# Short attention units: probabilities normed on VectorE before their transposition, in place of an inverse row fetched through DRAM

## The reference

```
B, T, M, D, G, H = 2, 1024, 256, 128, 4, 4
q = rope(einsum('bim,ghmd->bghid', x, w_aq)); k = rope(einsum('bim,gmd->bgid', x, w_ak))
v = einsum('bim,gmd->bgid', x, w_av)
s = einsum('bghid,bgjd->bghij', q * D ** -0.25, k * D ** -0.25)
s = s - 1e30 * (i < j)
p = softmax(s, axis=-1)
o = einsum('bghij,bgjd->bghid', p, v)
r = einsum('bghid,ghdm->bim', o, w_ao)
x = layernorm(x + r)
x = layernorm(x + moe(x))
```

## Time and profile before

| | |
|---|---|
| three runs | 1063.52 to 1064.9 us, median 1064.26 us |
| the profiled execution | 1066.87 us, span of its instructions 1065.0 us |
| TensorE's clock, mean of the span | 0.958 of full speed |
| busy share of the span | PE 89%, DVE 67%, ACT 49%, POOL 42% |

### The profile page before, as it was taken

How to read it: one execution, slowest core, us unless ns; L and a number is a source line. 1 busy time by engine, 2 the same in 40 slices (tenths; PEclk the granted TensorE clock), 3 DMA queues, 4 the chain that set the end, 5 groups by cost and what they waited for, 6 DMA issues and landing times.

```text
span 1065.0 us, 17542 instructions
## 1 busy us (share of the span) xinstructions
PE 950.3 (89%) x5448; PEld 733.9 (69%) x5448; DVE 710.2 (67%) x1751; ACT 517.4 (49%) x1139; POOL 447.2 (42%) x390
## 2 busy tenths in 40 slices
PE   8999996979999999999968899999999999478744
PEld 6887875756788878777756667888778777245411
DVE  5989863757767676767657877677777676433326
ACT  4111133545656656565656556556566655134402
POOL 3878872244342414124257534424132231325711
PEclk9999998989999999999999999999999999679968
DMA  8786766422334211211234235321212033999687
GB/s 241 234 265 226 258 227 178 131 94 78 99 88 121 64 50 46 68 40 61 66 103 122 71 95 135 92 75 42 70 42 61 26 108 87 257 260 224 87 280 285
DMA packets 137306, 137.28 MB, mean 129 GB/s; under 512 B 18065, under 2 KB 108805, under 8 KB 137216
## 3 DMA queue, kind: packets, MB, share of 16 engines
q1 hardware_dynamic: 84064, 98.33, 30.0%
q10 hardware_dynamic: 43872, 29.50, 9.3%
q0 software_dynamic: 9280, 8.34, 4.2%
HBM read 86.44 MB, written 63.05 MB: 140 GB/s over the span
## 4 chain that ended last, share of the span: by engine, by line
PE 68%; DVE 9%; issue 7%; DMA 7%; POOL 3%; SPq 3%; ACT 2%; ACTq 1%; POOLq 0%; DVEq 0%
PE s_ps L1193 16%; PE ring L1203 10%; PE o_ps L1223 10%; PE o_ps L1220 7%; PE s_ps L1172 6%; PE ring L1242 6%; PE ring L1172 5%; DMA sums<-erow,goal_u 3%; SPq L811 2%; PE o_ps L1172 2%; DVE neg_max L1407 2%; PE ring L1233 2%; PE s_ps L1196 1%; POOL slot_rows L909 1%; DMA fsum<-sums 1%
## 5 line engine op out<-in xcount | busy, mean ns | idle before, releaser
L1038 ACT ACTIVATE probs<-s_ps,neg_max 128x128 f32<-128x128 f32 (+7 forms) x256 | 189.4, 740 | 118.8 <-DVE neg_max L1407 110.4
L1193 PE MATMUL s_ps<-kt,qt_hi 128*128 128x512 f32 (+3 forms) x768 | 230.9, 382 | 5.1 <-issue 2.4
L1407 DVE TENSOR_REDUCE neg_max<-s_ps 128x1 f32<-128x128 f32 (+7 forms) x256 | 191.5, 751 | 57.4 <-PE s_ps L1196 55.6
L1203 PE MATMUL ring<-ident,probs 128*128 128x128 f32 x1152 | 177.1, 277 | 19.1 <-ACT probs L1038 10.4
L1193 PEld LDWEIGHTS s_ps<-kt,qt_hi 128*128 128x128 f32 x768 | 137.4, 192 | 50.5 <-issue 29.4
L938 ACT ACTIVATE pt_hi<-ring 128x512 fp32r<-128x512 f32 x168 | 100.1, 596 | 141.1 <-PE ring L1203 138.6
L881 POOL TENSOR_TENSOR ot_lo<-ot_raw,ot_hi 128x512 fp32r<-128x512 f32 x52 | 66.7, 1283 | 240.1 <-ACT ot_hi L938 240.1
L1341 DVE TENSOR_TENSOR pt_lo<-ring,pt_hi 128x512 fp32r<-128x512 f32 x168 | 115.6, 689 | 67.9 <-ACT pt_hi L938 65.4
L1203 PEld LDWEIGHTS ring<-ident,probs 128*128 128x128 f32 x1152 | 128.8, 142 | 43.6 <-issue 24.3
L1223 PE MATMUL o_ps<-pt_hi,v 128*128 128x512 f32 x336 | 144.2, 430 | 0.0
L886 POOL TENSOR_TENSOR qt_lo<-q_raw,qt_hi 128x512 fp32r<-128x512 f32 x64 | 82.3, 1286 | 130.9 <-ACT qt_hi L938 130.5
(11 more groups left out here) (211 smaller groups left out, 1576.2 us busy)
## 6 DMA issues: line engine op xcount, KB each, us to landing
qk_rows<-prods SPq DMA_DIRECT2D x80, 256.0 KB, 2.8
q_raw<-qk_rows ACTq DMA_DIRECT2D x128, 128.0 KB, 2.9
inv_row<-inverses SPq DMA_DIRECT2D x64, 256.0 KB, 3.6
fsum<-sums SPq DMA_DIRECT2D x48, 256.0 KB, 8.0
sums<-blank SPq DMA_DIRECT2D x16, 640.0 KB, 5.0
wexp<-in_L_ffn_w_gate_dram SPq DMA_DIRECT2D x32, 192.0 KB, 5.0
wexp<-in_L_ffn_w_up_dram SPq DMA_DIRECT2D x32, 192.0 KB, 5.3
wexp<-in_L_ffn_w_down_dram SPq DMA_DIRECT2D x32, 192.0 KB, 5.8
```

The source lines that it names most:

```text
L1038: act.activation(probs[:, u % 2, h, 0:blocks(u) * P], s_ps[:, n % 2, score_cols(n)], ACT.Exp, bias=neg_max[:, n % 8:n % 8 + 1], accum_out= ...
L1193: pe.matmul(s_ps[:, n % 2, c + a:c + e], q[qp], k[kp][:, a:e], start=(qp == kp == 0), stop=(qp == 1 and not last))
L1203: ins = pe.transpose(bank(s)[:, h * P:(h + 1) * P], probs[:, u % 2, h, j * P:(j + 1) * P], ident[:, :])
L1407: dve.tensor_reduce(neg_max[:, n % 8:n % 8 + 1], s_ps[:, n % 2, score_cols(n)], AX_X, ALU.max, negate=True).then_inc(max_ready, 1)
```

## The change

For units of at most four blocks, DVE multiplies the probabilities themselves by the reciprocals, in place, at the unit's first `ptrans` step, and PE's transpositions wait for that (`inv_ready`). Their `omul` is a plain copy, and the store and the load of the inverses are left out for them. The longer units keep the old way; their waits are counted over the longer units alone.

```diff
+NORMED_FIRST = 4
+def normed_first(u):
+    return blocks(u) <= NORMED_FIRST
+def normed_later(u):
+    return sum(not normed_first(n) for n in range(u))
...
-                if s[0] == "ptrans" and s[2] == 0:
-                    u = s[1]
+                if s[0] == "ptrans" and s[2] == 0 and not normed_first(s[1]):
+                    u, n = s[1], normed_later(s[1])
                     sp.wait_ge(inv_ready, u + 1)
-                    used(sp, inv_loaded[u % 2], 16 * (u // 2))
+                    used(sp, inv_loaded[u % 2], 16 * (n // 2))
...
-                    sp.wait_ge(inv_stored, 64 * (u + 1))
+                    sp.wait_ge(inv_stored, 64 * (n + 1))
...
                     pe.wait_ge(probs_ready, H * (u + 1))
+                    if normed_first(u):
+                        pe.wait_ge(inv_ready, u + 1)
                     for h in range(H):
...
                     dve.wait_ge(probs_ready, H * (u + 1))
-                    used(dve, inv_stored, 64 * (u - 1))
+                    used(dve, inv_stored, 64 * (normed_later(u) - 1))
                     after(dve.reciprocal(inv_sum[:, u % 2, 0:H], row_sum[:, u % 2, :]))
-                    dve.transpose(inv_t[:, u % 2, :], inv_sum[:, u % 2, :]).then_inc(inv_ready, 1)
+                    if normed_first(u):
+                        raw = probs[:, u % 2, :, 0:blocks(u) * P]
+                        dve.tensor_tensor(raw, raw, each(inv_sum[:, u % 2, 0:H], blocks(u) * P), ALU.mult
+                                          ).then_inc(inv_ready, 1)
+                    else:
+                        dve.transpose(inv_t[:, u % 2, :], inv_sum[:, u % 2, :]).then_inc(inv_ready, 1)
...
-                    dve.wait_ge(inv_loaded[u % 2], 16 * (u // 2 + 1))
                     dve.wait_ge(pv_done, PT_AT[(u, blocks(u) - 1)] + 1)
                     used(dve, attn_ready, u - 1)
-                    dve.tensor_tensor(ot_raw[:, u % 2, :], o_ps[:, :], inv_row[:, u % 2, :], ALU.mult).then_inc(o_ready, 1)
+                    if normed_first(u):
+                        dve.tensor_copy(ot_raw[:, u % 2, :], o_ps[:, :]).then_inc(o_ready, 1)
+                    else:
+                        dve.wait_ge(inv_loaded[u % 2], 16 * (normed_later(u) // 2 + 1))
+                        dve.tensor_tensor(ot_raw[:, u % 2, :], o_ps[:, :], inv_row[:, u % 2, :], ALU.mult
+                                          ).then_inc(o_ready, 1)
```

## The result

The changed kernel takes 1204.19 us (median of four runs, 1203.26 to 1205.24), the kernel before 1063.89 us (four runs, 1057.7 to 1064.9). The ratio is 1.1328, with an interval from 1.13 to 1.1356: 140 us slower, 48 us more than forecast and above the range.

What follows compares the result with a forecast made beforehand. PE's in-order execution was taken as the bound nearly everywhere in the short tiles. Waits 85 + GpSimd 6 + clock 12 - start 11 = +92 us, onto 1064.26 us: 1156 us; range 1112 to 1190 us.

Steps and rivals of the forecast that it cites:

- The mechanism: At each short unit's first transposition PE waits, in order, for DVE's multiplication: 32 waits, 76 to 116 us in all.
- The replaced waits: In the short tiles, new waits replace PE's old idle time: 31 us, besides the 8.56 us at the start.
- The multiplication: On DVE, 32 multiplications of probabilities, 0.68 to 2.32 us each by blocks, 48 us; GpSimd's hold-up adds 6 us.
- the clock: Half clock on PE after new waits in the 16 units of three and four blocks: 12 us taken.
- my middle: Price if all 16 units of three and four blocks lose 1.65 us each to half clock: 26 us.
- The upper bound that I named: Half clock in the 16 units of three and four blocks, each stretch lasting twice as long: twice 26 us.
- my three signs of being wrong: Transpositions do not wait; multiplication well below 0.53 us per block; PE's other idle time shrinks by more than 31 us.
- The start: First batch's start: 8.56 us of PE idle time and 3.0 us of half clock removed, 11 us gained.
- The one called lag and clock: Rival: DVE's lag stays and the clock falls at every long wait; +140 us, 1204 us; chance 0.12.
- GpSimd's hold: Rival: GpSimd holds up nearly every multiplication, 41 us in place of 6; +127, 1191 us; chance 0.07.
- The rival in which new waits only replace old ones: In short tiles, all 31 us of old idle time go and the clock holds; +34, 1098 us; chance 0.15.
- The two cases on the other side: Faster, multiplication ready when PE arrives: -11, 1053 us, chance 0.04; no difference, waits and start cancelling: chance 0.02.

## Why the prediction was wrong, point by point

*The mechanism was right.* PE's transpositions wait 32 times, 118.0 us in all, which I had put between 76 and 116 us before contention and at 122 with 6 us for it. The tiles of five to eight blocks are as long as before: 229.0 and 228.5 us hold the steps that took 228 each.

*The replaced waits were nearly right.* I let them take all of the 39.3 us of old idle time; 9.5 us of other idle time are left, so 29.8 went, the 8.56 us of the start among them. Net idle time is +88.2 us, by my terms 116 + 6 - 39.3 = 83.

*The multiplication was right.* 53.9 us for the 32 by the four shapes, of which 48 were priced as work and 6 as GpSimd's doing. In unit 13 the multiplication takes 4.08 us in place of 2.29, and GpSimd's row beside it shows what for:

```profile
314.52 1.28 POOL L899 TENSOR_TENSOR qt_lo<-q_raw,qt_hi 128x512 fp32r<-128x512 f32 x1
```

The subtraction ends at 315.80 us, the multiplication at 317.96 us, 2.16 us later, about its own length. All of the 6 us lie in nine multiplications that ran beside a two-input operation of GpSimd on `qt_lo` (one on `prods` as well); the other 23 are within 0.01 us of the shortest of their shape. In unit 45 the multiplication of 2.29 us, from 769.32 us, was not held up, and the subtraction took 2.54 us in place of 1.28:

```profile
770.20 2.54 POOL L899 TENSOR_TENSOR qt_lo<-q_raw,qt_hi 128x512 fp32r<-128x512 f32 x1
```

The Trainium skill ("SBUF — State Buffer", section "SBUF: two separate sides") has this as a lock that whichever starts first holds for its whole length. This trace agrees that one of the two stands until the other is through. Who holds it cannot be told from the starts of the records: in unit 13 the multiplication's record starts 0.64 us ahead of the subtraction's, while GpSimd was at an indirect DMA, and it was the multiplication that was held up. The copy out of PSUM costs 0.692 us against 0.689, as priced.

*The step that failed is the clock:* "I take 12 us, half of the middle, since not every wait will do it". PE's busy time grew by 51.4 us for the same work; with the 3 us that I credited at the start, the forecast had it at +9. That is 42 of the 48 us by which it fell short; the other 6 are idle time, 88 us where 82 were forecast (85 + 6 - 8.56). I had taken from the earlier trace rows that a wait of about 2.4 us sometimes halves the clock, counted only the 16 units of three and four blocks, and then halved the price. From the first transposition of unit 0 to that of unit 8, and from unit 32 to unit 40, it is almost only units of one and two blocks that run; before and after:

```profile
155.47:209.77 54.30, 42.83 (x249) 34.00 (x249) 26.22 (x93) 26.90 (x88) 14.74 (x14) 0.91 0.54 158
534.14:594.91 60.77, 46.66 (x302) 36.93 (x302) 43.52 (x142) 35.26 (x101) 39.21 (x33) 0.97 0.37 109
```

```profile
153.91:229.00 75.09, 52.57 (x249) 41.62 (x249) 39.11 (x97) 29.15 (x89) 17.73 (x15) 0.79 0.30 90
598.89:691.96 93.07, 60.05 (x301) 47.67 (x301) 51.72 (x142) 36.65 (x102) 42.69 (x34) 0.76 0.18 53
```

PE is busy for 23 us more in them, where I had put nothing. The other 28 us fell to the units of three and four blocks, where my middle was 26 and I took 12. At the start, where I had expected 1.00, the clock is 0.50 from 156.0 to 176.3 us, with waits of 1.28 us (unit 1) and 1.83 us (unit 2). The upper bound that I named, twice 26 us, comes to the measured price by luck: it let the half clock of 16 units last twice as long, while nearly half of the price lay in the other 16. I did not carry it into the range either, and none of my three signs of being wrong was the clock's.

*The start was mis-sized for the same reason.* I credited 11 us for it. The 8.56 us did go, but four waits with half clock behind them took their place. The run with the first four units alone gives +0.3 us for both together; where the clock was kept, the start was worth 8.8 and 9.6 us.

*The rivals.* The one called lag and clock gave 1204 us, the time that came, but by two errors of 28 us that cancel. For idle time it had 116 + 9 - 8.56 us, where 88 came: it left the other 31 us of old idle time in place, of which 21 went, and it had 125 us of new waits, where 118.0 came. For the clock it had 26 - 3 us, where 51 came. That DVE catches up while PE stands, which I held against it, is not so: 118.0 less the 53.9 us of multiplications leaves 64 us for lag and signals, which I had read as 65 + 3. DVE stands too, for PE's next scores, and the steps of the routing come up again ahead of the second head's maximum, as in unit 12. GpSimd's hold is 6 us and not 41. The rival in which new waits only replace old ones fell by both of its conditions: the waits came to 118.0 us and not 76, and the clock did not hold. The two cases on the other side fell by the row of 32 waits.

## What to carry to other kernels

An in-order engine that is the bound pays for a wait twice where its clock follows its activity: for the time that it stands, and for the work behind it. Price both from rows, and take the price of the second from every wait, also from the short ones between short pieces of work: here they brought 23 of the 51 us. When work is moved to an engine with room, look at what stands ahead of it in that engine's order: here half of the loss came with hardly any work, and the same work, put earlier and for the four units where a transfer was really waited for, made the kernel 0.8% faster.

## What the runs showed of the hardware

Waits of 1.6 to 2.3 us, one in each of four units of some 5 to 8 us, held the clock at 0.66 on average from 155 to 180 us; waits of 0.55 to 1.23 us in units of some 3 to 4 us left it at 1.00. The length of a wait alone did not tell: 2.41 us left it at 1.00 before.

GpSimd's issue of an indirect DMA is held up by the multiplication as well. Beside the one of 2.29 us at 297.17 us it took 3.09 us (again 3.09 us in unit 44), the next one 0.97 us:

```profile
297.23 3.09 POOL L922 DMA_INDIRECT slot_rows<-row,slot_u  x1 [1.43 <-DVE slot_u L1559]
300.63 0.97 POOL L922 DMA_INDIRECT slot_rows<-row,slot_u  x1 [0.30 <-issue]
```
